# Twelve-head attention: the value product stands behind the first tile's scores, in a bank of the other pair

## The reference, cut to what matters

```python
x2 = _ln(x, ln1_g, ln1_b)
qkv = x2 @ in_proj_w.T + in_proj_b            # q, k, v: 12 heads of 16
scores = einsum('bqhd,bkhd->bhqk', q, k) / sqrt(16)
ao = einsum('bhqk,bkhd->bqhd', softmax(scores), v).reshape(B, S, D)
x = x + ao @ out_proj_w.T + out_proj_b
xm = _ln(x, ln2_g, ln2_b)                     # router: top 2 of 8 experts, then the experts
```

## Time and profile before

| what | value |
|---|---|
| median of three timed runs | 2086.38 us |
| the profiled execution (span) | 2106.3 us |
| mean granted TensorE clock | 0.822 of full speed |
| stage of the change, first scores to last turned scores | 1236.0 to 1680 us |
| bodies that hold a first half | 16 |

### The profile page before, as it was taken

How to read it: one execution, slowest core, us unless ns; L and a number is a source line. 1 busy time by engine, 2 the same in 40 slices (tenths; PEclk the granted TensorE clock), 3 DMA queues, 4 the chain that set the end, 5 groups by cost and what they waited for, 6 DMA issues and landing times.

```text
span 2106.3 us, 35471 instructions
## 1 busy us (share of the span) xinstructions
PE 1611.5 (77%) x12060; PEld 1159.8 (55%) x12060; DVE 1312.3 (62%) x4361; ACT 979.3 (46%) x2773; POOL 400.4 (19%) x494
## 2 busy tenths in 40 slices
PE   0166764968888578888888768888888759999996
PEld 0032223855665355555555456666676647777775
DVE  7898885878888677877788536555555532122221
ACT  1366998933444445554555323333333324443442
POOL 7302331000000100000000001222212223333332
PEclk9975555578888689999999878777777769999998
DMA  3000001079910000000000000000000037777775
GB/s 71 15 1 1 1 1 20 3 141 193 188 20 0 1 1 0 0 0 0 0 0 0 1 25 13 24 23 23 23 15 19 23 96 179 185 175 181 177 176 133
DMA packets 136262, 112.99 MB, mean 54 GB/s; under 512 B 29417, under 2 KB 128457, under 8 KB 136137
## 3 DMA queue, kind: packets, MB, share of 16 engines
q1 hardware_dynamic: 119320, 91.70, 18.4%
q0 software_dynamic: 16864, 20.33, 5.0%
HBM read 69.19 MB, written 45.94 MB: 55 GB/s over the span
## 4 chain that ended last, share of the span: by engine, by line
PE 52%; DVE 27%; ACT 14%; issue 4%; POOL 1%; DVEq 0%; DMA 0%; another core or an unknown queue 0%; SPq 0%; ACTq 0%; POOLq 0%
ACT bank L716 8%; PE bank L2322 8%; PE bank L1007 6%; PE bank L2307 5%; PE bank L2311 3%; PE bank L1987 3%; PE bank L966 3%; PE bank L1217 2%; PE bank L1665 2%; PE bank L1000 2%; PE bank L2000 2%; DVE WK L1839 1%; DVE WK L1581 1%; DVE R L1581 1%; DVE R L1839 1%
## 5 line engine op out<-in xcount | busy, mean ns | idle before, releaser
L1047 POOL TENSOR_TENSOR WK<-WK,mhalf 128x2 f32<-128x2 f32 (+1 forms) x96 | 77.9, 812 | 882.4 <-DVE WK L1505 328.4
L2359 ACT ACTIVATE R<-bank,R 128x256 f32<-128x256 f32 x234 | 98.2, 471 | 216.9 <-PE bank L2311 216.9
L2211 DVE SCALAR_TENSOR_TENSOR WK<-bank,R,WK 128x192 f32<-128x192 f32 x78 | 28.9, 413 | 262.8 <-PE bank L2322 262.8
L716 ACT ACTIVATE bank<-bank,nbias,sc 128x128 f32<-128x128 f32 x384 | 168.9, 991 | 22.6 <-POOL nbias L528 22.6
L1007 PE MATMUL bank<-WK,R 96*128 96x256 f32 x576 | 162.9, 429 | 17.0 <-ACT WK L973 11.0
L2240 POOL DMA_INDIRECT moe_sum<-WK x78 | 121.5, 1557 | 257.4 <-DVE WK L2211 196.4
L2322 PE MATMUL bank<-R 128*128 128x192 f32 x936 | 169.1, 331 | 0.0
L716 ACT ACTIVATION_READ_ACCUMULATOR bank<-bank,nbias,sc 128x1 f32 x384 | 163.0, 766 | 0.0
L2322 PEld LDWEIGHTS bank<-R 128*128 128x128 f32 x936 | 150.1, 190 | 13.3 <-issue 13.3
L1007 PEld LDWEIGHTS bank<-WK,R 96*128 96x128 f32 x576 | 116.2, 213 | 41.9 <-ACT WK L973 15.4
L2307 PE MATMUL bank<-R 128*128 128x256 f32 x468 | 125.2, 390 | 1.1 <-ACT R L2350 1.1
(11 more groups left out here) (494 smaller groups left out, 3886.4 us busy)
## 6 DMA issues: line engine op xcount, KB each, us to landing
moe_rows_in<-zeros SPq DMA_DIRECT2D x1, 25026.0 KB, 138.7
R<-in_L_ffn_w SPq DMA_DIRECT2D x39, 576.0 KB
R<-in_L_ffn_w SPq DMA_DIRECT2D x39, 384.0 KB
R<-moe_rows_in SPq DMA_DIRECT2D x39, 194.0 KB, 4.6
R<-in_L_ffn_w SPq DMA_DIRECT2D x78, 96.0 KB
R<-in_L_ffn_b SPq DMA_DIRECT2D x39, 96.0 KB
moe_sum<-resid POOLq DMA_DIRECT2D x16, 192.0 KB
moe_sum<-WK POOLq DMA_INDIRECT x78, 5.9
```

The source lines that it names most:

```text
L716: ins = nc.scalar.activation(s, s, ACT.Exp, bias=nbias[:, u, k:k + 1], scale=col(SS), accum_out=units(sum_all, g, u)[:, k:k + 1])
L2359: ins = nc.scalar.activation(x_hid[q], bank[(0, 2, 0)[p] + n][:, 0:NR], ACT.Gelu, bias=xb_1[h][:, q:q + 1])
```

## The change: what it does

The value product leaves the place between the third feature product and the scores of tile 0, and is issued after the scores of tile 0 and after the other stream's projection, ahead of the wait for the row maxima. It writes bank 1 of the **other** stream, which is free there: that bank's turned attention output has been copied out before the projection. VectorE's v add moves from before the row maxima of tile 0 to before those of tile 1, behind the other stream's projection, residual and statistics. The scores of tile 0 no longer wait for the v add; the wait for it stands before the product with v. The wait for the routing's position (`f.r_pos`) stays in front of the scores. The number of `yield`s is the same.

```diff
@@ vector_m_1
                 placed(v, ch, g, a, f)
+            row_tops(v, g, a, f, 0)
+            yield
             v.wait_ge(f.v_p, per(g, 1, 1))
             for i in range(M):
-                ins = nc.vector.tensor_tensor(a.m_va[:, i, :, 0:DH], heads(a.bank[0][:, i * D:(i + 1) * D]), heads(mb_v),
-                                              ALU.add)
+                ins = nc.vector.tensor_tensor(a.m_va[:, i, :, 0:DH], heads(other(a).bank[1][:, i * D:(i + 1) * D]),
+                                              heads(mb_v), ALU.add)
             ins.then_inc(f.v, 1)
-            row_tops(v, g, a, f, 0)
-            yield
             row_tops(v, g, a, f, 1)
@@ new
+        def other(a):
+            return streams[1 - a.n]
+        def values_beside(a, f):
+            for i in range(M):
+                for c in range(2):
+                    mm = nc.tensor.matmul(other(a).bank[1][:, i * D:(i + 1) * D], a.xT[0:C, c, i * P:(i + 1) * P],
+                                          mw_v[0:C, c, :], start=(c == 0), stop=(c == 1))
+            mm.then_inc(f.v_p, 1)
@@ tensor_m_1
             m_features(a, f, 1)
+            yield
             if prev:
                 pe.wait_ge(f.r_pos, per(g, 1, 0))
-            token_product(a, mw_v, 0, f.v_p)
-            yield
             pe.wait_ge(f.qk, per(g, 3, 3))
-            pe.wait_ge(f.v, per(g, 1, 1))
             scores(pe, g, a, f, 0, f.scores, False)
             yield
+            values_beside(a, f)
             pe.wait_ge(f.rowmax, per(g, 4 * M, 4))
             scores(pe, g, a, f, 1, f.scores, False)
...
             pe.wait_ge(f.exp, per(g, 4 * M, 5))
+            pe.wait_ge(f.v, per(g, 1, 1))
             m_times_v(a, f, 0)
```

## The result

The change makes the kernel faster: 2053.38 us against 2086.39 us before (medians of four runs each), a ratio of 0.9848 with a 95% interval of 0.9834 to 0.9862. That is 33 us; the forecast was 7.4 us, and the time lies under the range (2062 to 2097). The direction was right, the size was not. Once more, on another chip, the same kernel had 0.9868 (0.9851 to 0.9885).

What follows compares the result with a forecast made beforehand. No engine alone but a hand-over between them was taken to bound the kernel; -1.09 + 0.63 = -0.46 us a body over 16 bodies gave -7.4 us, from 2086.4 to 2079.0 us, range 2062 to 2097.

Steps and rivals of the forecast that it cites:

- The scores' earlier start: Scores of tile 0 follow ScalarE's q and k copies, not the v add: 1.09 us earlier in each body.
- The v add on VectorE's path: Moved between statistics and row maxima of tile 1, where VectorE has no hole, the v add costs 0.63 us a body.
- The value product for nothing in TensorE's hole: Placed in TensorE's 1.57 us wait for the row maxima of tile 0, the product of 1.57 us costs 0.00.
- The unknown, the late completions: With sends, maxima start 2.01 us after scores, without 1.01; the forecast let this lateness move with the scores.
- Rival A: Completions tied to the sends: maxima of tile 0 stay, the v add costs 0.63 in 14 bodies; +7.9, 2094.3 us; chance 0.25.
- the sum itself: Per body -1.09 + 0.63 = -0.46 us, times 16 bodies: -7.4 us, forecast 2079.0 us; chance 0.38.
- full success in both lateness and clock: The range's low end: it was to reach beyond the clock gain, priced as 16 x -1.46 = -23.4, 2063 us.
- rival C: Filling TensorE's hole keeps the clock up; longer bodies become as the shorter: 11.9 us more gain, 2067 us; chance 0.15.
- The sign that I named for it: A mean clock of the attention stage away from 0.75 by over 0.03 would show a clock effect.
- Rival B: Late completion of the value product delays the v add on VectorE; the 0.46 gain is gone, 2086.4 us; chance 0.14.
- Rival D: Shorter bodies move the clock's changes and its rise comes later: +11.9 - 7.4, 2091 us; chance 0.08.

Runs made afterwards that it cites:

- second profile of before: The kernel before the change, unedited, profiled once more: span 2081.9 us, timed median 2082.6 us, ratio 0.9998.
- first profile: The kernel before the change, as profiled for the prediction: span 2106.3 us, 19.9 us over the median of its timed runs (2086.4 us).
- fill alone: The kernel before, plus a second value product that nobody reads in TensorE's hole behind the projection: 2082.8 us, ratio 0.9998.
- product in front with fill: The changed kernel with VectorE's new order, value product again in front of the scores, and an unread product in the hole: 2083.9 us, ratio 0.9997.
- bank alone: The kernel before, value product in its old place but in the other stream's bank 0, scores not waiting for the v add: 2078.5 us, ratio 0.9977.
- two adds more: The changed kernel with two more unread adds on VectorE ahead of the v add: 2085.0 us, ratio 0.9984.
- front product, new order: The changed kernel with VectorE's new order, value product again in front of the scores, in the other stream's bank 0: 2086.3 us, ratio 1.0018.

## Why the prediction was wrong, by its own steps

*The scores' earlier start, -1.09 a body.* Right: from the end of the features to the maxima of tile 0 the bodies take 3.11 us in the second profile of before and 1.95 after, -1.16.

*The v add on VectorE's path, +0.63.* Right in place, a little too dear: from the maxima of tile 0 to those of tile 1 it is 3.46 us in the second profile of before and 3.99 after, +0.53. Together the path falls from 6.58 to 5.96, -0.62 where I had -0.46. This term was a little small, not the one that failed.

*The value product for nothing in TensorE's hole.* Right for the wrong reason. The hole that I measured, 1.57 us, was that of the first profile; in the second it is 0.57. Scores 1 start 3.68 us after scores 0, before 3.01. VectorE's longer way hides it: it reaches the maxima of tile 1 1.33 us after scores 1 have started, and 1.01 is what the scores need.

*The unknown, the late completions.* Not a property of the kernel. The first profile had them, in 14 bodies, the second and all the runs behind it had none. The sign was there: the profiled span lay 19.9 us over the timed median. I carried it along as an offset "that I leave as it is" instead of asking which rows held it, and then built a rival (A, 0.25) and half of the range on them. The second profile's mean body is 1.69 us shorter (28.95 to 27.26), 22 us over 13 bodies, about the offset. What made the completions late in that execution is open. Rival A is out for the changed kernel: its maxima start at 1461.19, before the third DMA of the sends (1462.50 in its timeline). All the later profiles have 1.01 to 1.12 us from scores to maxima, with and without sends. The rule of the Trainium skill that I weighed ("SBUF — State Buffer", in "SBUF: two separate sides": TensorE waits for nobody there) agrees with these profiles.

*The step that failed is the sum itself:* that 16 bodies times a shorter path is the gain, with nothing for the clock in the rest of the body. 13 bodies x 0.62 = 8 us. The bodies became 27.26 - 25.23 = 2.03 us shorter, 26 us over the same 13. The other 18 us lie in the rest, where the change moved no instruction: 20.7 us in the second profile of before, 19.3 after, while the half clock in it fell from 11.3 to 6.6 us. The same 13 bodies as one window, before (second profile) and after, each from the third to the sixteenth start of the maxima of tile 0:

```profile
1287.62:1642.00 354.38, 299.72 (x2861) 243.08 (x2862) 214.31 (x853) 134.98 (x312) 86.39 (x104) 0.79 0.07 22
```

```profile
1285.01:1613.00 327.99, 274.19 (x2861) 220.65 (x2861) 212.91 (x852) 133.22 (x312) 86.54 (x105) 0.87 0.07 24
```

TensorE runs 2861 instructions in both and is busy 25.5 us less; VectorE is busy 1.4 us less. What the half clock costs an instruction: the turned scores take 1.66 us at 0.50 and 0.95 at 1.00, the router's product 1.88 and 1.06.

The turned scores and the router's product in the second profile of before (half clock), then in the changed kernel (full clock), timeline:

```profile
1459.70 1.88 PE L2066 MATMUL bank<-R,WK 96*128 96x8 f32 x8
...
1461.51 1.66 PE L1987 MATMUL bank<-WK 32*128 32x128 f32 x24
```

```profile
1443.82 1.06 PE L2078 MATMUL bank<-R,WK 96*128 96x8 f32 x8
...
1445.59 0.95 PE L1987 MATMUL bank<-WK 32*128 32x128 f32 x24 [0.71 <-ACT R L2119]
```

*The range was added up wrongly at its low end.* It was to hold full success in both lateness and clock, but 16 x -1.46 = -23.4, 2063, is the lateness alone. With the 11.9 us of rival C it would have been 2051. That the measured 2053.4 lies just above this would have been luck in part, since there was no lateness to lose.

*Rival C had the mechanism and not the size.* It said that the filled hole keeps TensorE busy ahead of the clock's fall, priced it at 11.9 us on top of the forecast, 2067, and gave it 0.15. The sign that I named for it, a clock over 0.03 away from 0.75, came (0.89 and 0.86), though the second profile of before would have given it as well (0.79 and 0.78). The price was wrong because I took the better of the two streams' bodies (28.20 us) as the best that there can be; the new bodies (25.50 and 25.83) are both under it. Its argument against, that the hole around the maxima of tile 1 stays, was true and did not matter. That a filled hole alone would do it is also wrong: fill alone 2082.8, product in front with fill 2083.9. In these runs the large gain needs both conditions: short path with the hole empty 2073.6, long path with the hole filled 2085.0, both together 2053 to 2064. Rival B didn't occur: in the changed kernel VectorE never waits for the value product. Rival D, a clock that takes back what a shorter path gives, is seen in small in "bank alone" (0.43 us off the path, 0.16 back on the rest).

*What stays open.* Six kernels with paths of 6.49 to 6.80 us and different holes have a mean body of 27.3 to 27.4 us. In two of them, "two adds more" and "front product, new order", full and half clock alternate every 13.65 us, 27.31 us for the pair, and the mean body has 27.32. They are in step. That the other four fall into step in the same way is argued, not shown. Nor does a given time at half clock always cost the same: with 13.65 us the rest is 20.3 to 21.0 us in "front product, new order" and 21.9 to 22.0 in the second profile of before. The runs don't show by what rule the clock falls, so the place of the step between 6.23 and 6.49 could not have been forecast from them.

## What to carry to other kernels

Where the TensorE clock changes inside a loop, a term on the path is not worth its own length: here 0.26 us in a loop of 16 cost more than 20 us, and the same filler gave 0 or 14.5 us. So read the clock by body first, forecast a jump as a case of its own, and test an edit by adding a little work on its path and by filling the hole with work that nobody reads. And reconcile the profiled span with the timed median before using any row: find which rows hold the difference, or profile once more.

## What the runs showed of the hardware that was not expected

Taking 1.5 us of matmuls out of each body made the kernel some 17 us slower (0.9948 against 0.9868), with TensorE's clock at half for 12.6 us of a body instead of 6.6 to 7.4. Adding matmuls whose output nobody reads made one kernel 14.5 us faster (2078.5 to 2064.0). A program at the edge of the two patterns gave 2059.2 us in one run and 2088.1 in another, on the same chip. One program ran the same 154 matrix instructions of a body's rest in 17.23 us with no half clock and in 19.71 with 10.24 us of it. One execution showed TensorE's completions 0.9 us late or more in 14 bodies, a second one of the same program in none.
